# Level 5 of a delta-rule attention kernel's key and query products in pairs of column tiles, with a new order on all engines

## The reference, cut to what matters

```python
q = short_conv(x @ Wq.T, wq_conv); k = short_conv(x @ Wk.T, wk_conv); v = short_conv(x @ Wv.T, wv_conv)
q = scale ** 2 * _rmsn(q, EPS_QK); k = scale * _rmsn(k, EPS_QK)
g = -jnp.exp(A_log) * jax.nn.softplus(x @ Wfa.T @ Wfb.T + dt_bias)
beta = jax.nn.sigmoid(x @ Wb.T)
def step(S, inputs):
    q_t, k_t, v_t, g_t, b_t = inputs
    S = S * jnp.exp(g_t)[..., None]
    delta = b_t[..., None] * (v_t - jnp.einsum('bhd,bhdv->bhv', k_t, S))
    S = S + k_t[..., None] * delta[:, :, None, :]
    return (S, jnp.einsum('bhd,bhdv->bhv', q_t, S))
out = _rmsn(out, EPS_NORM) * o_norm_w * jax.nn.sigmoid(x @ Wga.T @ Wgb.T)
```

## Time and profile before

| | |
|---|---|
| median of 3 runs | 5065.29 us (5062.55 to 5066.39) |
| the profiled execution | 5056.96 us, its span 5055.0 us |
| TensorE clock granted, mean | 0.992 of full |
| busy: PE, DVE, ACT, POOL | 93%, 74%, 66%, 57% of the span |
| the 128 steps of the attention | 52.8 to about 4154 us of the span |
| behind them | the experts, to 5055 us, which the change doesn't touch |

### The profile page before, as it was taken

How to read it: one execution, slowest core, us unless ns; L and a number is a source line. 1 busy time by engine, 2 the same in 40 slices (tenths; PEclk the granted TensorE clock), 3 DMA queues, 4 the chain that set the end, 5 groups by cost and what they waited for, 6 DMA issues and landing times.

```text
span 5055.0 us, 111131 instructions
## 1 busy us (share of the span) xinstructions
PE 4725.1 (93%) x28928; PEld 3607.3 (71%) x28928; DVE 3754.1 (74%) x8897; ACT 3339.2 (66%) x7216; POOL 2881.8 (57%) x6210
## 2 busy tenths in 40 slices
PE   6999999999999999999999999999999997999999
PEld 4777777777777777777777777777777775555555
DVE  5878787778787778887777888777888773555555
ACT  5777777777777777777777777777777772111111
POOL 4767676667676667676667776767676761000000
PEclk8999999999999999999999999999999998999999
DMA  2211111111111111111111111111111110000000
GB/s 83 62 37 37 37 37 37 34 35 38 36 37 35 38 37 37 37 37 33 35 37 36 36 37 37 37 37 37 33 37 35 37 31 31 13 8 12 8 12 13
DMA packets 213962, 172.58 MB, mean 34 GB/s; under 512 B 146272, under 2 KB 163936, under 8 KB 213216
## 3 DMA queue, kind: packets, MB, share of 16 engines
q1 hardware_dynamic: 213344, 165.49, 11.5%
HBM read 119.03 MB, written 46.40 MB: 33 GB/s over the span
## 4 chain that ended last, share of the span: by engine, by line
PE 62%; ACT 19%; issue 11%; POOL 4%; DVE 2%; DMA 1%; POOLq 0%; SPq 0%; ACTq 0%; DVEq 0%
PE bank L1593 10%; PE bank L1384 8%; PE bank L1285 7%; PE bank L1432 4%; PE bank L1603 4%; PE bank L1406 4%; PE bank L1362 4%; ACT L642 3%; ACT lx L578 3%; PE bank L1337 2%; PE bank L1437 2%; PE bank L1293 2%; PE bank L1419 2%; ACT T L588 2%; ACT e_sb L638 2%
## 5 line engine op out<-in xcount | busy, mean ns | idle before, releaser
L1384 PE MATMUL bank<-kq,kl 128*128 128x128 f32 x6144 | 852.9, 281 | 48.2 <-DVE kq L883 40.4
L391 POOL TENSOR_TENSOR kl<-kl,tot 128x256 f32<-128x256 f32 x768 | 510.1, 664 | 565.0 <-PE bank L1384 563.7
L1384 PEld LDWEIGHTS bank<-kq,kl 128*128 128x128 f32 x6144 | 749.7, 191 | 108.9 <-issue 71.4
L1285 PE MATMUL bank<-xT,par 128*128 128x512 f32 x1536 | 750.2, 598 | 0.4 <-ACT bexp L535 0.4
L414 POOL TENSOR_TENSOR rm<-rm,mul 32x14 f32<-32x14 f32 (+6 forms) x1792 | 512.7, 286 | 141.1 <-POOL mul L410 0.8
L410 POOL TENSOR_TENSOR mul<-pm,rm 32x14 f32<-32x14 f32 (+6 forms) x1792 | 522.7, 292 | 107.4 <-issue 6.6
L883 DVE TENSOR_TENSOR kq<-kq,tot 128x512 f32<-128x512 f32 x768 | 537.4, 700 | 0.0
L893 DVE COPY_PREDICATED AT<-mask,bank 128x256 f32<-128x256 uint32 x896 | 468.0, 522 | 0.1
L371 POOL TENSOR_TENSOR rstd<-rstd,minus_half 128x4 f32<-128x4 f32 x32 | 32.3, 1008 | 738.1 <-DVE rstd L828 738.1
L801 ACT ACTIVATE q<-bank 128x512 f32<-128x512 f32 x144 | 86.0, 597 | 522.1 <-PE bank L1593 522.1
L1406 PE MATMUL bank<-T,lx 128*128 128x64 f32 x3072 | 387.1, 269 | 4.2 <-issue 4.1
(11 more groups left out here) (176 smaller groups left out, 12486.1 us busy)
## 6 DMA issues: line engine op xcount, KB each, us to landing
par<-params_dram SPq DMA_DIRECT2D x128, 519.0 KB, 3.3
blocks_out<-lx SPq DMA_DIRECT2D x128, 256.0 KB, 2.0
lx<-blocks_in SPq DMA_DIRECT2D x128, 256.0 KB, 2.7
pm<-blocks_out SPq DMA_DIRECT2D x512, 8.0 KB
blocks_in<-rm SPq DMA_DIRECT2D x512, 8.0 KB
out_dram<-xall SPq DMA_DIRECT2D x16, 512.0 KB, 2.9
xall<-x_dram SPq DMA_DIRECT2D x5, 1536.0 KB, 7.1
lx<-ffn_dram SPq DMA_DIRECT2D x1, 3456.0 KB, 11.0
```

Source lines behind the costliest of these rows:

```text
L391: pool.tensor_tensor(halves(kl[:, :], w)[:, :, 0, :], src, totr.broadcast_to([P, SEQ // (2 * w), w]), ALU.mult).then_inc(s["kl_ready"], 1)
L1285: ins = pe.matmul(bank[t][:, :], par[p][:, at:at + P], chunk(xT, kt, SEQ), start=kt == 0, stop=kt == KT - 1)
L1384: ins = pe.matmul(dst[:, :, n], chunk(left, n), right[:, :, n, :, 1, :], start=True, stop=True)
```

## The change

Level 5 (w = 32) is no longer one matmul per chunk with 128 columns of weights and 128 of moving data, but two: one for each pair of blocks, with the 32 tokens of the left block as weights and 2 x 32 moving columns, written to partitions 0 to 31 and 64 to 95. The other levels stay. And in `step` of PE, ACT, DVE, POOL and SP the calls are put in another order. No other function changes.

```diff
+TILED = 5
@@ SP
-                if B:
-                    next_params()
                 if D:
                     blocks_from_pool()
                     diagonals_back()
...
                 next_x()
+                if B:
+                    next_params()
@@ POOL
                     eliminate(iD, 10)
+                    eliminate(iD, 11)
                 if B:
                     kl_update(0)
                 if D:
-                    eliminate(iD, 11)
                     eliminate(iD, 12)
...
                     kl_update(3)
+                    kl_update(4)
                 if A:
                     totals(1)
...
                     totals(4)
-                if B:
-                    kl_update(4)
-                if A:
                     totals(5)
-                    totals(6)
-                    totals(7)
-                next_rstd()
                 if B:
                     kl_update(5)
...
                     eliminate(iB, 2)
+                if A:
+                    totals(6)
+                if B:
+                    eliminate(iB, 3)
                     kl_update(6)
-                    eliminate(iB, 3)
+                next_rstd()
...
                     eliminate(iB, 6)
+                if A:
+                    totals(7)
@@ ACT
+                if C:
+                    w_evict(0)
+                if A:
+                    tap0(0, "q_mm")
                 if B:
                     k_copy()
-                if C:
-                    w_evict(0)
-                if A:
-                    tap0(0, "q_mm")
+                if A:
+                    tap0(1, "k_mm")
                 if C:
                     w_evict(1)
                 if A:
-                    tap0(1, "k_mm")
                     softplus_exp()
                     softplus_max()
                     softplus_ln()
+                if C:
+                    w_evict(2)
+                if A:
                     tap0(2, "v_mm")
-                if C:
-                    w_evict(2)
                 if D:
                     t16_scale()
...
                     lt16_scale()
-                if A:
-                    decay()
...
                     tt16_evict()
-                if C:
-                    w_evict(3)
-                if D:
                     x_evict(4)
                 if N:
                     turned_x(nb, 1)
+                if C:
+                    w_evict(3)
+                if A:
+                    decay()
+                if N:
+                    fa_evict(nb)
+                if C:
+                    output_squares()
                 if A:
                     silu(0)
                     silu(1)
-                if C:
-                    output_squares()
...
@@ DVE
+                if A:
+                    conv(0, 1)
                 if C:
                     s_update(0)
                 if A:
-                    conv(0, 1)
+                    conv(0, 2)
                 if C:
                     residual(1)
                 if A:
-                    conv(0, 2)
                     conv(0, 3)
+                    conv(1, 1)
                 if B:
                     l_evict(1)
                     qk_evict(1)
-                if A:
-                    conv(1, 1)
                 if C:
                     s_update(1)
...
+                if B:
+                    l_evict(5)
+                if C:
+                    output_moments()
+                if B:
+                    kq_update(5)
                 if A:
                     kq_init(1)
...
                     qk_evict(5)
+                if C:
+                    outputs()
                 if D:
                     t_update(5)
-                if C:
-                    outputs()
...
@@ PE
+                    if l == TILED:
+                        pe.sem_inc(s["pe_go"], 1)
                     for n in range(NCH):
-                        ins = pe.matmul(dst[:, :, n], chunk(left, n), right[:, :, n, :, 1, :], start=True, stop=True)
+                        if l != TILED:
+                            ins = pe.matmul(dst[:, :, n], chunk(left, n), right[:, :, n, :, 1, :], start=True, stop=True)
+                            continue
+                        for m in range(HALF // w):
+                            at = 2 * w * m
+                            ins = pe.matmul(dst[at:at + w, :, n, m], left[:, n * P + at:n * P + at + w],
+                                            right[:, :, n, m, 1, :], start=True, stop=True)
                     ins.then_inc(s["lvl_mm"], 1)
...
+                if B:
+                    level(0)
                 if C:
                     solve(0)
-                if B:
-                    level(0)
...
                 if B:
                     level(5)
                 if D:
                     turn_t(4)
                     lt_times_t(5)
+                if A:
+                    project_g(3)
+                if B:
+                    turn_v()
                 if N:
                     next_ga(nb)
                 if D:
                     t_products(5)
                 if B:
-                    turn_v()
                     level(6)
                 if D:
                     turn_t(5)
+                if C:
+                    turn_og()
+                if D:
                     lt_times_t(6)
-                if C:
-                    turn_og()
                 if N:
                     next_beta(nb)
                 if A:
                     sums()
-                if D:
-                    t_products(6)
                 if C:
                     project_out(0)
                     project_out(1)
+                if D:
+                    t_products(6)
```

More of the change, by code:

```diff
@@ L712, in turned_k @@
                     act.activation(kT[pB][:, :], b_x[:, 0:3 * P], ACT.Copy).then_inc(s["kt_ev"], 1)
-                if B:
-                    k_copy()
                 if C:
@@ L719, in step @@
                     tap0(0, "q_mm")
+                if B:
+                    k_copy()
+                if A:
+                    tap0(1, "k_mm")
                 if C:
@@ L726, in step @@
                     softplus_ln()
-                    tap0(2, "v_mm")
                 if C:
                     w_evict(2)
+                if A:
+                    tap0(2, "v_mm")
                 if D:
                     t16_scale()
+                if N:
+                    turned_x(nb, 0)
                 if B:
                     lt16_scale()
+                if D:
+                    tt16_evict()
+                    x_evict(4)
+                if N:
+                    turned_x(nb, 1)
+                if C:
+                    w_evict(3)
                 if A:
@@ L736, in step @@
                 if N:
-                    turned_x(nb, 0)
-                if D:
-                    tt16_evict()
+                    fa_evict(nb)
                 if C:
-                    w_evict(3)
-                if D:
-                    x_evict(4)
-                if N:
-                    turned_x(nb, 1)
+                    output_squares()
                 if A:
@@ L748, in step @@
                     silu(1)
-                if C:
-                    output_squares()
-                if N:
-                    fa_evict(nb)
                 if D:
@@ L764, in step @@
                     square(1)
+                if N:
+                    ga_evict(nb)
                 if D:
                     tt_evict(5)
-                    x_evict(6)
                 if C:
                     turned_og()
+                if D:
+                    x_evict(6)
                 if A:
@@ L1048, in step @@
                     softplus_one()
+                if C:
+                    residual(2)
+                if A:
                     softplus_rest()
@@ L1071, in step @@
                     residual(3)
-                next_moments()
+                if A:
+                    conv(2, 1)
+                    conv(2, 2)
+                    conv(2, 3)
                 if B:
@@ L1076, in step @@
                     kq_update(4)
-                if A:
-                    conv(2, 2)
                 if D:
                     t_update(4)
-                if A:
-                    kq_init(1)
-                    conv(2, 3)
                 if B:
@@ L1089, in step @@
                     kq_update(5)
+                if A:
+                    kq_init(1)
+                if B:
                     qk_evict(5)
+                if C:
+                    outputs()
                 if D:
                     t_update(5)
-                if C:
-                    outputs()
                 if B:
                     l_evict(6)
+                next_moments()
+                if B:
                     kq_update(6)
@@ L1100, in step @@
                 next_scale()
-                if D:
-                    t_update(6)
                 if B:
@@ L1107, in step @@
                     residual_stream(1)
```

(30 more changed lines are left out.)

14 lines of the change are left out of this document (3 added, 11 removed).

## The result

The changed kernel takes 4972.77 us (median of 4 runs, 4969.52 to 4974.84) against 5063.92 before (4 runs, 5059.44 to 5066.39): 0.9821 of the time, 95% interval 0.9805 to 0.9837, so 91 us less. The forecast was 4955, with a range of 4900 to 5035.

The account below looks back on a forecast made before the run. The prediction took a ring of waits through PE, DVE and ACT as the bound, not PE's work. 96 us from ordinary steps and 10 from N steps gave 106 less, 4959 as median, taken as 4955; range 4900 to 5035.

Parts of the forecast that it names:

- The ring: Whole step: PE and DVE to project_f, ACT to sums_evict, mutual waits undone by reordering; 30.67 us a step, from 31.53.
- Half the gain: Rival, chance 0.22: just-in-time arrivals late by 0.2 to 0.4 us on the ring; 31.1 us a step, 5010.
- The tiling is worth nothing: Level 5 on PE: tiled 0.9 us against 0.95, hidden within 1.4 us free; about nothing in N steps too.
- the lower bound: Tiled level 5 on PE: 8 overlapping pairs of passes at 0.054 us each, 0.43, before the cost of tiles.
- the 1.4 us of cover: PE from level 5's start at 18.85 to x_evict(5)'s end at 22.2: level 5 may take 1.4 us without moving anything.
- Edits at nothing: Moves costed at nothing, such as next_params and eliminate(11) ahead of kl_update(0), giving level 1 its operand 0.65 us later.
- the forecast's own signs: Forecast wrong if ACT waits for PE or DMA in its stretch, level 5 exceeds 1.9 us, or POOL is late for level 1.
- The N steps: The 15 longer steps of 127, filled mostly by PE's work: 35.7 us instead of 36.37, 0.65 less each.
- The sum: All steps: 112 x 0.86 + 15 x 0.65 = 106 us less.
- Slower by the tiles: Rival, chance 0.08: level 5's small tiles each pay a whole weight load, 3.4 us; step 32.1, 76 us slower, 5140.

Follow-up runs that it names:

- the cover restored: Changed kernel with totals(1) waiting for kq_update(4), totals(4) and totals(5) behind the first eliminations, eliminate(11) behind kl_update(0): 4961.77 us, 0.98 of the kernel before.
- the edit above: Changed kernel with one call moved on POOL, eliminate(11) back behind kl_update(0): 4955.27 us, 0.9788 of the kernel before.

## Why the prediction was right, and where it wasn't

**The ring.** That PE and DVE lead up to `project_f`, ACT takes over, and PE closes the step behind `square(1)`, held in every kernel with the new order on all engines, but for the one in which `totals(1)` waits alone. From `softplus_exp` to `square(1)` it is 17.93 us, 18.04 forecast, and with the cover restored or level 4 in tiles no head position's median fell under 30.6. `softplus_exp` starts at 7.55 in three of the seven ordinary head positions, exactly as forecast, and those steps take 30.69, against 30.67; in three others it starts 0.14 to 0.22 later, and they take 30.82 to 30.94 (why, wasn't followed up); the seventh, h = 6, is below. The 0.02 between 30.69 and 30.67 is partly luck. `sums` was to start 0.06 behind the end of `square(1)` and starts 0.23 behind it. The rows had that already: 1985.36 + 0.64 = 1986.00 in the earlier trace rows, and 1986.24 in the earlier trace rows. The stretch on ACT, 0.11 shorter, and the groups behind `sums`, 4.33 instead of 4.38, make up for it. Half the gain, the likeliest rival, asked for late arrivals of 0.4 us on the ring in every step; there was one of that size, in one head of eight.

**The tiling is worth nothing: wrong.** It is worth 46 us in the new order (0.34 a step) and 12.6 in the old. Two numbers of that step failed. The first is the start of level 5, 18.85 forecast and 19.77 measured. 0.23 of the 0.92 is level 4, which ends at 17.53, not 17.3. 0.44 is `kq_update(4)`, costed at 0.68 from the earlier trace rows and taking 1.12 beside `totals(1)` on POOL. And 0.24 is the time from the end of `kq_update(4)` to PE's first pass, which the forecast left out; it is the same with tiles and without (0.78 and 0.79 of wait). POOL's calls were moved without asking what runs beside them on DVE. The Trainium skill (SBUF — State Buffer, SBUF: two separate sides) says that a VectorE instruction with two SBUF inputs and a GpSimd instruction that reads SBUF exclude each other for their whole length. The trace agrees in kind, by 1.12 against 0.68 for `kq_update(4)`. It doesn't show the whole length: the record grows by 0.44 where `totals(1)` had 0.57 to go, and the 1.39 us of `norms` lengthened nothing on DVE.

The second is level 5's length, 0.76 to 1.19 forecast and 0.57 measured. From the first pass to the last it is 0.42, as the lower bound's 0.43 for pairs that overlap. But the bound added 0.33 from `sums` for going into tiles and out. The way out, from the last pass to `turn_t(4)`, is 0.15; the way in is covered by the wait for DVE, and where PE comes straight from another group (tiles in the old order) it is 0.20 instead of 0.11 to the first pass. So the way in costs 0.09. The way out costs 0.04 to 0.05 more than the 0.11 between two passes, so that of the 0.33 some 0.14 is left. The 0.20 that the forecast read for the way in from `sums` was the wait for `square(1)`: `sums` starts 0.24 behind its end there. Nor does `pe_go` hold the tiles back: in the old order their first pass is at 1979.73, before the record of the group ahead of it ends, at 1979.80.

The two errors nearly cancel in the number, and that is luck: a level 5 that starts 0.92 late and is 0.33 shorter than the 0.9 taken still brings `t_products(5)` to 22.38 (22.2 forecast), because 0.5 of the 1.4 us of cover was to spare. They don't cancel in the explanation. The forecast gave all 106 us to the order, and the order alone gives 46. Without tiles the late level 5 stands on the ring, as the run of the order alone showed.

**The h = 6 step.** `eliminate(11)` ahead of `kl_update(0)` was costed at nothing in *Edits at nothing*, with level 1's operand at about 5.0. Behind the step with `next_rstd` it comes at 5.65 (4.81 and 0.84), and the step gains 0.18 instead of 0.86: 15 x 0.68 = 10 us short of the sum, of which the edit above gave 8 back. By the forecast's own signs (wrong if POOL is late for level 1) it failed there.

**The N steps.** 8 of the 15 take 35.20 us, 0.5 less than forecast. The other 7 take 36.84, which makes the mean 35.97 and the gain 0.37 instead of 0.65 each, 4 us short. Windows over one of the long ones, and over the stretch in another where it differs (the third number from the end is the granted clock); then PE there:

```profile
3531.22:3568.06 36.84, 36.37 (x244) 28.06 (x242) 26.65 (x61) 26.82 (x59) 23.51 (x53) 0.95 0.12 32
...
1787.00:1790.00 3.00, 3.00 (x11) 1.85 (x6) 0.16 (x1) 0.92 (x3) 1.66 (x7) 0.56 0.00 0
```

```profile
1787.72 3.49 PE L1368 MATMUL bank<-wo_sb,lx 128*128 128x256 f32 x8
1791.05 1.00 PE L1451 MATMUL bank<-TT,lx 128*128 128x64 f32 x8
```

`project_out` takes 3.33 us instead of 1.83. The granted clock is at its lower level for most of that, 1.2 GHz instead of 2.4, and PE had no wait ahead of it, with `next_beta`'s 16 passes of 8 columns and `sums` just before. Costs: 1.64 us for each, 11 in all. None of the 15 N steps of the kernel before shows it. With the tiles in the old order one does (38.67 instead of 36.99, a granted clock of 0.75 from 1828 to 1831 us), so it doesn't take the new order. The number differs between kernels with the same PE order, and in the second profile of the changed kernel it is 8. Why it falls there in some N steps stays open; no run was made for it.

**The sum.** 106 us were forecast and 85.8 measured in the attention; the front is 2.5 shorter, what lies behind it 4.2 longer. Of the 20 that are missing, 10 are the h = 6 steps' and 4 the N steps'; the other ordinary steps, 0.61 to 1.03 shorter by head position, are 6 us short of 0.86 each. *Slower by the tiles* fell: at 0.028 us a pass, weights load beside running passes.

## What to carry to other kernels

Look for the engine whose work between two fixed points nothing can shorten, and count it; ACT's 17.9 us told the step within 0.2 us or so, while what PE's own edits were worth depended on who was late ahead of them. When calls move on POOL or DVE, ask also what then runs beside them on the other. Orders of several engines are one edit: change them together, and leave a wait off an engine whose next results are due at once, even where it is idle for much of the span.

## What the runs showed of the hardware

- fp32 matmuls with 32 columns of weights and 64 moving, on two column tiles, follow each other at 0.028 us (15 gaps in 0.42). 32 passes with 16 columns and 32 moving, on four tiles, took 0.44 us with the way out. A full pass of 128 columns takes 0.11. The weight loads of the changed kernel's level 5, in one step:

```profile
L1397 PEld LDWEIGHTS bank<-kq,kl x16: 106/110/110, 1935.5 to 1935.9; 128*32 128x32 f32 x16
```

  A load's record lasts 0.11 us and the next begins 0.028 later, so by the records about four are under way at once.
- `zz` on DVE, 4 columns wide, took 0.58 us where it began 0.06 behind POOL's `kl_update`, and 0.16 where it began between two of POOL's (`totals(1)` waiting): by the records, a small instruction can wait for nearly all of a large one of the other engine.
- The granted clock fell for some 3 us in 7 of 15 steps with the same instructions and in the other 8 not; in another execution of the same kernel it was 8 and 7.
